# A two-layer graph kernel: z taken from x itself, W0 applied where z is turned, and the first four rows of z accumulated side by side

## What is computed

```
A = adj (4096 x 4096), x (4096 x 128)
scale = sum over k of d[k] * filt[k] * d[k]                 # one number per row
x1  = layernorm(x  + A @ (scale * (A @ (x @ W0))) + bias)
z2  = (A / rowsum(A)) @ x1 @ W_in;  y = (A.T / colsum(A)) @ x1 @ W_out
out = layernorm(x1 + z2 + y)
```

## Time and profile before

| | |
|---|---|
| median of 3 runs | 744.5 us (744.1 to 745.57) |
| profiled execution, its own time | 744.1 us |
| its span, by the profile | 742.3 us |
| PE busy | 732.4 us (99%) |
| weight loads busy | 606.3 us (82%) |
| DVE busy | 551.9 us (74%) |
| ACT busy | 476.1 us (64%) |
| POOL busy | 1.9 us |
| moved by DMA | 208.64 MB, mean 281 GB/s |
| granted TensorE clock, mean | 0.997 |

### The profile page before, as it was taken

How to read it: one execution, slowest core, us unless ns; L and a number is a source line. 1 busy time by engine, 2 the same in 40 slices (tenths; PEclk the granted TensorE clock), 3 DMA queues, 4 the chain that set the end, 5 groups by cost and what they waited for, 6 DMA issues and landing times.

```text
span 742.3 us, 9053 instructions
## 1 busy us (share of the span) xinstructions
PE 732.4 (99%) x3337; PEld 606.3 (82%) x3337; DVE 551.9 (74%) x669; ACT 476.1 (64%) x1167; POOL 1.9 (0%) x8
## 2 busy tenths in 40 slices
PE   8999999999999999999999999999999999999996
PEld 6878888888888888888888888888888888888885
DVE  5896865838474455887665647988897999899996
ACT  6897673837264534334343346999998888777772
POOL 0000000000000000000000000000000000000000
PEclk9999999999999999999999999999999999999998
DMA  9998875765556446255555559999989999999991
GB/s 367 394 367 349 358 268 215 260 220 205 217 202 226 158 182 226 87 206 209 179 177 217 173 191 377 385 384 383 378 328 385 386 371 373 375 365 354 352 357 34
DMA packets 35244, 208.64 MB, mean 281 GB/s; under 512 B 3584, under 2 KB 8448, under 8 KB 10752
## 3 DMA queue, kind: packets, MB, share of 16 engines
q1 hardware_dynamic: 34640, 207.34, 74.2%
q10 hardware_dynamic: 560, 0.72, 0.3%
HBM read 205.95 MB, written 2.10 MB: 280 GB/s over the span
## 4 chain that ended last, share of the span: by engine, by line
PE 95%; ACT 2%; DVE 1%; DMA 1%; issue 0%; SPq 0%; DVEq 0%
PE accA L594 15%; PE accA L591 15%; PE accA L600 15%; PE accB L591 12%; PE accB L594 12%; PE accB L600 12%; PE accC L594 4%; PE accC L591 4%; PE accC L600 4%; PE nat L615 2%; ACT hi L280 2%; PE nat L622 1%; PE nat L632 1%; DMA raw<-in_adjT_b 1%; DVE rows L503 0%
## 5 line engine op out<-in xcount | busy, mean ns | idle before, releaser
L398 DVE TENSOR_TENSOR lo<-raw,hi 128x2048 fp32r<-128x2048 f32 x184 | 417.4, 2288 | 134.6 <-ACT hi L280 103.0
L280 ACT ACTIVATE hi<-raw 128x512 fp32r<-128x512 f32 x512 | 315.6, 620 | 65.4 <-DMA raw<-in_adjT_b 37.9
L591 PE MATMUL accA<-hi,x_hi 128*128 128x512 f32 x512 | 201.5, 394 | 0.8 <-ACT x_hi L288 0.8
L594 PE MATMUL accA<-hi,x_lo 128*128 128x512 f32 x512 | 199.5, 390 | 0.3 <-DVE x_lo L403 0.3
L283 ACT ACTIVATE hi<-raw 128x2048 fp32r<-128x2048 f32 x64 | 122.1, 1912 | 66.9 <-DMA raw<-in_adjT_b 66.8
L600 PE MATMUL accA<-lo,x_hi 128*128 128x512 f32 x512 | 137.1, 390 | 0.6 <-DVE lo L398 0.6
L591 PEld LDWEIGHTS accA<-hi,x_hi 128*128 128x128 f32 x512 | 96.2, 188 | 20.9 <-ACT x_hi L288 1.1
L600 PEld LDWEIGHTS accA<-lo,x_hi 128*128 128x128 f32 x512 | 95.9, 188 | 21.0 <-DVE lo L398 1.1
L594 PEld LDWEIGHTS accA<-hi,x_lo 128*128 128x128 f32 x512 | 96.2, 188 | 19.8 <-DVE x_lo L403 0.6
L591 PE MATMUL accB<-hi,v_hi 128*128 128x512 f32 x256 | 100.5, 393 | 0.2 <-DVE v_lo L432 0.2
L594 PE MATMUL accB<-hi,v_lo 128*128 128x512 f32 x256 | 99.7, 389 | 0.0
(11 more groups left out here) (72 smaller groups left out, 462.6 us busy)
## 6 DMA issues: line engine op xcount, KB each, us to landing
raw<-in_adjT_b SPq DMA_DIRECT2D x127, 1024.0 KB, 5.4
raw<-in_adj_b SPq DMA_DIRECT2D x64, 1024.0 KB, 6.0
rows<-in_xT_b SPq DMA_DIRECT2D x8, 256.0 KB, 8.8
rows<-in_x_t SPq DMA_DIRECT2D x8, 256.0 KB, 6.9
out<-rows SPq DMA_DIRECT2D x7, 256.0 KB, 7.1
raw<-in_adjT_b SPq DMA_DIRECT2D x1, 512.0 KB, 5.3
raw<-in_adjT_b ACTq DMA_DIRECT2D x1, 512.0 KB, 5.4
out<-rows SPq DMA_DIRECT2D x1, 128.0 KB, 1.8
```

The source lines that it names most:

```text
L280: nc.scalar.activation(hi[slot][:, t], raw[slot][:, t], ACT.Copy, accum_out=sums[:, TPB * K + t, C:C + 1]).then_inc(s_hi, 1)
L398: nc.vector.tensor_tensor(lo[slot][:], raw[slot][:], hi[slot][:], ALU.subtract).then_inc(s_lo, 1)
L591: nc.tensor.matmul(acc, r_hi[:, TPB * K + t], h[:, t], start=(first and t == 0), stop=False)
L594: nc.tensor.matmul(acc, r_lo[:, TPB * K + t], h[:, t], start=False, stop=False)
```

## The change

1. `x_w0`, `xT_b`, the loads of `xT_b` and the later load of `x_t` go. Each block of x is loaded once (`load_x`), and x itself is split. ACT makes `x_hi` (`x_first`), POOL makes `x_lo`; DVE does both for block 0 (`x_start`).
2. At turning, z is multiplied by W0 (`by_rows(I, w0)`) where it was transposed. `v_block` is divided: ACT makes `v_hi` (`v_first`, four scaled 128x128), DVE makes `v_lo` with four fused instructions.
3. Rows 0 to 3 of z (LEAD = 4) run in step: for each block J of x, the chunks (J, 0), (J, 1), (J, 2), (J, 3), into four accumulators. The last two J come row by row. These 32 chunks give z only. The row sums are not taken there.
4. The 10 o products of those rows with J <= I move to phase 2, whose list gets 10 more chunks ("alone": they give an o product and nothing else), set between those that give o and y ("both"). The sums of A are taken in phase 2 instead: there every chunk is split tile by tile.
5. The first two chunks are loaded by tile (three tiles of them from ACT's queue), the next 14 in halves; `lo` of the first 32 chunks is made in quarters or halves.
6. Semaphore counts, positions and the place of one `inverse` follow.

```
+LEAD = 4
-    phase1 = [((I + 1 + k) % NB, I) for I in range(NB) for k in range(NB)]
-    phase2 = [(J, I) for I in range(NB - 2, -1, -1) for J in range(NB - 1, I, -1)]
+    lead = [(J, I) for J in range(NB - 2) for I in range(LEAD)]
+    lead += [(J, I) for I in range(LEAD) for J in (NB - 2, NB - 1)]
+    phase1 = lead + [((I + 1 + k) % NB, I) for I in range(LEAD, NB) for k in range(NB)]
+    phase2 = []
+    for I in range(NB - 2, -1, -1):
+        both, alone = list(range(NB - 1, I, -1)), list(range(I + 1)) if I < LEAD else []
+        while both or alone:
+            if alone:
+                phase2.append((alone.pop(0), I))
+            if len(both) > 1 or not alone:
+                phase2.append((both.pop(0), I))
...
-    y_behind = {N1 + 3: [N1]}
-    for n in range(N1 + 4, N2):
+    both = [n for n in range(N1, N2) if chunks[n][0] > chunks[n][1]]
+    y_behind = {both[3]: both[:1]}
+    for n in both[4:]:
         done = sum(len(m) for m in y_behind.values())
-        many = 2 if n == N1 + 6 else 1
-        y_behind[n] = list(range(N1 + done, N1 + done + many))
+        many = 2 if n == both[6] else 1
+        y_behind[n] = both[done:done + many]
...
+    turn1 = {28: 0}
+    for I in range(1, NB - 1):
+        turn1[LEAD * NB + I if I < LEAD else last1[I] + 2] = I
+    v_from = {n + 2: turn1[n] for n in turn1}
...
+    TILEWISE, HALVES = range(2), range(2, 4 * LEAD)
+    parts = [TPB if n in TILEWISE else 2 if n < LEAD * NB else 1 for n in range(N4)]
...
+        z_acc = [accA[:, 0], accA[:, 1], accC[:, 0], accC[:, 1]][:LEAD]
+        z_acc += [accA[:, I % 2] for I in range(LEAD, NB)]
...
+            def load_x(b):
+                sp.dma_start(rows[:, block_of(b)], x_t[:, block_of(b)]).then_inc(s_x[b], 16)
...
+            def v_first(I):
+                if I == 0:
+                    act.wait_ge(s_sc, 1)
+                act.wait_ge(s_n, I + 1)
+                for t in range(TPB):
+                    row = TPB * I + t
+                    last = nc.scalar.activation(v_hi[:, row], nat[:, I % 2, P * t:P * t + P], ACT.Identity,
+                                                scale=scale[:, row:row + 1])
+                last.then_inc(s_vhi, 1)
...
+            def x_first(b):
+                act.wait_ge(s_x[b], 16)
+                nc.scalar.activation(x_hi[:, block_of(b)], rows[:, block_of(b)], ACT.Copy).then_inc(s_xhi, 1)
...
+            for b in range(1, NB):
+                pool.wait_ge(s_xhi, b)
+                nc.gpsimd.tensor_tensor(x_lo[:, block_of(b)], rows[:, block_of(b)], x_hi[:, block_of(b)],
+                                        ALU.subtract).then_inc(s_xlo, 1)
...
             def v_block(I):
+                dve.wait_ge(s_vhi, I + 1)
                 for t in range(TPB):
+                    row = TPB * I + t
+                    last = nc.vector.scalar_tensor_tensor(v_lo[:, row], nat[:, I % 2, P * t:P * t + P],
+                                                          scale[:, row:row + 1], v_hi[:, row], ALU.mult, ALU.subtract)
+                last.then_inc(s_v, 1)
...
             def turn_z(I):
                 pe.wait_ge(s_tz, I + 1)
                 if I == 0:
                     pe.wait_ge(s_small, 16 * len(small))
-                transposes(NAT_Z + I, I)
+                by_rows(I, w0)
```

More of the change, by code:

```diff
@@ L88, in graph_kernel @@
     for n in range(N1):
-        if chunks[n][0] != chunks[n][1] and n not in HELD:
+        if not held(n):
             ranked(n)
         if n in diag1:
-            ranked(NB * diag1[n] + NB - 1)
+            ranked(last1[diag1[n]])
     for n in HELD + [N1 - 1]:
@@ L95, in graph_kernel @@
     for n in range(N1, N2):
+        if n not in both:
+            ranked(n)
         for m in y_behind.get(n, []):
@@ L105, in graph_kernel, with with_sums @@
         slot = n if n < RING else slot_of[order[n - RING]]
-        landings[slot] += 16 if n else 0
+        landings[slot] += 0 if n in TILEWISE else 16
         slot_of.append(slot)
         landed.append(landings[slot])
+    def with_sums(n):
+        J, I = chunks[n]
+        return J <= I and I >= LEAD if n < N1 else n < N2 or is_z2[n]
     hi_at, lo_at = [], []
@@ L269, in _, with split @@
         def _(act):
-            def split(n, tiles=range(TPB)):
+            def split(n):
                 slot = slot_of[n]
                 K, C = chunks[n]
-                if n:
+                if n not in TILEWISE and n not in HALVES:
                     act.wait_ge(s_raw[slot], landed[n])
-                if n < N1 or is_z2[n]:
-                    for t in tiles:
-                        if n == 0:
-                            act.wait_ge(s_piece[t // 2], 16)
+                if with_sums(n):
+                    to = sums[:, 1 if is_z2[n] else 0]
+                    for t in range(TPB):
@@ L280, in split @@
                         nc.scalar.activation(hi[slot][:, t], raw[slot][:, t], ACT.Copy,
-                                             accum_out=sums[:, TPB * K + t, C:C + 1]).then_inc(s_hi, 1)
+                                             accum_out=to[:, TPB * K + t, C:C + 1]).then_inc(s_hi, 1)
+                elif n < LEAD * NB:
+                    for t in range(TPB):
+                        if n in TILEWISE:
+                            act.wait_ge(s_tile[n][t], 16)
+                        elif n in HALVES and t == 0:
+                            act.wait_ge(s_half[slot], landed[n])
+                        elif n in HALVES and t == 2:
+                            act.wait_ge(s_raw[slot], landed[n])
+                        nc.scalar.activation(hi[slot][:, t], raw[slot][:, t], ACT.Copy).then_inc(s_hi, 1)
@@ L587, in product, with by_hi @@
                 h, l = hi[slot_of[n]], lo[slot_of[n]]
-                for t in range(TPB):
+                def by_hi(t):
                     if t == 0 or hi_at[n][t] > hi_at[n][t - 1]:
@@ L621, in transposes @@
                     to = slice(P * t, P * t + P)
-                    mm = nc.tensor.transpose(nat[:, e % 2, to], turned[:, u % 2, to], ident[:])
-                mm.then_inc(s_n, 1)
-            def x_w0(n):
-                b = chunks[n][0]
-                pe.wait_ge(s_xT[b], 16)
-                if n == 0:
-                    pe.wait_ge(s_w0, 16)
-                room(n)
-                for t in range(TPB):
-                    mm = nc.tensor.matmul(nat[:, n % 2, P * t:P * t + P], rows[:, TPB * b + t], w0[:],
-                                          start=True, stop=True)
+                    mm = nc.tensor.transpose(nat[:, e % 2, to], turned[:, e % 2, to], ident[:])
                 mm.then_inc(s_n, 1)
```

271 lines of the change are left out of this document (138 added, 133 removed).

## The result

The changed kernel takes 746.95 us (median of 10 runs, 745.74 to 747.98), the one before 744.49 (10 runs beside them, 743.93 to 745.57): ratio 1.0028, 95% interval 1.002 to 1.0036. It is 2.5 us slower by the medians. I had forecast 741.5, with 0.12 for slower; 746.95 lies above my range. The profiled run took 745.86 us with a span of 743.7, against 744.1 and 742.3 before. What lies outside the span is 2.1 us here and was 1.8 before, so it isn't the same for both kernels as I had written: 0.3 us of the difference lies there.

The account below looks back on a forecast made before the run. PE was taken to bound the kernel. PE's work -2.9, lead -3.4, stall +3.4 gave -2.9 us, less 0.3 for the slow clock: -2.6 on 744.1, so 741.5 us, range 737.0 to 746.0.

Parts of the forecast that it names:

- the lead: First 32 chunks, one product each: 6.7 us of PE time lost where 10.1 were lost before, a gain of 3.4.
- slow clock at the start: Start of the run: 0.3 us left for PE's slow clock when it begins earlier.
- my formula: Lead: landing is 4 us, plus bytes beyond 0.68 MB at 418 GB/s, plus 0.7; chunk 23 lands at 67.7, ends 71.5.
- four chunks with an x block: Lead: their transfers take 10.7 us against PE's 10.9, so the lag hardly grows.
- -6.3 us of PE's work: Row 0: removing x W0 from PE counted as a saving of 6.3 us.
- PE's work, -2.9: Whole run: x W0 gone, -6.3 us; eight z blocks rise from 0.48 to 0.91, +3.4; sum -2.9 us.
- The stall at chunk 71: Phase 2: PE waits 3.4 us for `lo`, because DVE makes x1 of block 5 first.
- The later rows of phase 2: x1 of rows 4, 3, 2 ends before `lo` is wanted, two places with 1.0 us to spare: nil, bound +2.
- The transfers' steady rate: Lead: transfers deliver 418 GB/s with full queues, as in the trace from 4 to 28 us.
- POOL's `x_lo`: Lead: about 1.3 us per operation; delays to DVE cost 0.5 us, bounds 0 and 4.
- Rival 2: Lead served worse, by 395 GB/s transfers or POOL's 4 us: 3.6 us later, 745.1, no change; chance 0.21.
- Rival 3: Lead bound by transfers in earnest, 370 GB/s: 8.1 us late, 749.6, slower; chance 0.12.

Follow-up runs that it names:

- e12: e7 with ident, bias, w_out and w_in (0.26 MB) loaded behind chunks 36 to 39 instead of 18 to 21: 741.62 us, ratio 0.9954 to the kernel before.
- e7: Changed kernel with (7,3) first in row 3 of phase 2, x1 of block 4 and its square root one chunk earlier, `x_lo` on DVE: 742.37 us.
- e9: The kernel before without three of the four x W0 tiles of blocks 2 to 7, 4.1 us less PE work: 743.62 us, ratio 0.9984.
- e11: The kernel before without sums in the first 16 splits and without three of four x W0 tiles of blocks 2 to 7: 743.32 us, ratio 0.9976.
- e10: The kernel before without the sums in ACT's first 16 splits, x W0 whole: 743.17 us, ratio 0.9981.
- e3: Changed kernel with LEAD = 0: W0 at turning and quick start stay, phase 1 goes row by row: 745.76 us, ratio 1.0012 to the kernel before.
- e1: Changed kernel with (7,3) first and (0,3) second in row 3 of phase 2: 744.15 us, ratio 0.999 to the kernel before.
- e4: Changed kernel with `x_lo` of blocks 1 to 7 made by DVE instead of POOL, all bytes loaded: 746.58 us, ratio 1.0018 to the kernel before.
- e2: Changed kernel with chunks 6 to 31 loading two of their four tiles, each read twice: 756.84 us, ratio 1.0153 to the kernel before.
- e6: Changed kernel with chunks 6 to 31 loading two of four tiles and `x_lo` on DVE: 743.79 us, ratio 0.9983 to the kernel before.

## Why the prediction was wrong

**The step that failed** is the lead: "The lead costs 6.2 + 0.5 = 6.7 us of lost PE time", set against 10.1 before, a gain of 3.4. Its mechanism held (PE is fed by the transfers, at 419 GB/s behind the first 10 us, and its lost time stands behind the last block of x), its size did not: 11.0 us were lost, a cost of 0.9. 8.0 of them were there at product 4, where my numbers gave 6.2, and 3.0 were added up to product 25, where they gave nothing. In the profiled run the sum is then 741.5 + 4.3 (lead) + 0.1 (stall) - 0.3 (slow clock at the start, which did not come) + 0.3 (outside the span) = 745.9; it took 745.86. The parts of the 4.3, worked out at chunk 24, for which my formula gives a landing at 4 + (25 x 1.0486 + 8 x 0.262 - 0.68)/0.418 + 0.7 = 70.8 and an end at 74.6, 6.6 us lost (I had stopped at chunk 23, with 6.2):

- The first 10 us brought 0.48 MB less than I put: 1.15 us. I had taken the start's rates from another set of transfers, the kernel before's, and no tile of it was loaded by itself. No run isolates this term. I had also put PE's first matmul at 5.0 (5.60), but the transfers covered that.
- The small loads, 0.42 MB, go out with chunks 16 to 21, inside the stretch; I had counted them for chunk 34 only: 1.0 us. e12 shows it for 0.26 of the 0.42 MB.
- A landing is later than its bytes' turn. By 74.06 the stretches had moved 0.57 + 2.14 + 7.5 + 13.4 + 6.0 = 29.6 MB, and up to chunk 24 they needed 28.7: 0.9 MB of later chunks were in before it, 2.1 us, where I had allowed 0.7. That is 1.4, worked out, not isolated by a run.
- Between landing and PE's end 5.1 us instead of 3.8: 1.3. POOL, for which I had left 0.5, has 0.8 of them (e7 against the changed kernel): its `x_lo` and the operation queued behind it.
- The rate was 419 to 425 where I had 418, which gives back 0.35.

1.15 + 1.0 + 1.4 + 1.3 - 0.35 = 4.5, and 6.6 + 4.5 = 11.1, where 11.0 were measured. To my 6.7 that is 4.5 + 0.4 (chunk 24 for 23) - 0.5 (allowed for POOL) = 4.4.

**The reason behind it** is a sentence of mine: "four chunks with an x block take (4.19 + 0.26)/0.418 = 10.7 us and PE 10.9". At 98% use there is next to no reserve. What is late stays late, and I had added up only the delays that I could name at the start. The kernel before had a reserve: x W0 made row 0's pace 3.62 us a chunk against 3.13 of transfers. So "-6.3 us of PE's work" was an accounting that held for PE's work and not for the time: with 4.1 us of it taken away e9 won 1.2 us by its ratio and 0.3 by its span, and e11 nothing that shows against e10. e3 took all of it away and lost, though DVE and ACT's order had a share there. e9 also shows that the reserve was not lost evenly: 2.8 us were won up to product 7, and the landing of chunk 8 took them back.

**Right by its own steps.** PE's work, -2.9: measured. The stall at chunk 71, 3.4 us by DVE's order, with x1 of block 5 ahead of it: 3.5, and e1 takes it away. What I had no term for is the clock behind such a stall, 1.6 us more in e4's execution. The later rows of phase 2, which I put at nil: nothing more was lost there. But "at two places with 1.0 us to spare" held only for that order; e1 opened one of them for 1.7 us. The transfers' steady rate: 418 against 419 to 425. The slow clock at the start: the profile of the changed kernel has 1.00 in all stretches shown, so nothing for my 0.3.

**POOL's `x_lo`.** I had 1.3 us from the width of the row; it is 1.27 when DVE leaves it alone (the shortest in e2) and 1.81 to 2.22 beside it in the changed kernel. The Trainium skill (SBUF — State Buffer, "Who interferes with whom"), which I cited for two engines that shut each other out for an instruction, names what e4, e7 and e2 show; but I had thought of DVE as the loser in the main, and in e2 it is POOL, for 20 us.

**The rivals.** Rival 2, the lead served worse, came nearest, with a price of 3.6 us where 4.3 was true; of its two causes neither came as written (the rate was 357 GB/s from 4 to 10 us and not low all along, and POOL cost 0.8), and I had given it 0.21. The chances failed because of that: a sum that lives on a resource at 98% should have its own case of delays that add up, with more weight than the case in which all goes to plan. Rival 3's 370 GB/s did not come in the lead. What I held against it was in part wrong: "in those 22 us the ring was full and loads waited for releases" does not fit 28 to 30 us, where 199 GB/s were moved with chunks 8 to 10 already issued. Two small slips: at 428 GB/s the lead would be 1.5 us shorter, not 1.1, and at 391 it would be 4.3 longer, not 4.1; neither changes the forecast.

**The median and its spread.** The profiled run is 1.1 us faster than the median, and only so does the median lie above my range. The ten runs of the changed kernel spread from 745.7 to 748.0, those of e7 from 742.2 to 742.8. They fall in two groups: five with a mean granted clock of 0.997 took 745.7 to 746.7, five with 0.993 to 0.996 took 747.2 to 748.0. e4 shows the same two groups, at 744.7 to 745.2 and 746.2 to 747.6, and its profiled run, of the second, has the clock of 0.57 behind the stall. So the second group of the changed kernel is probably the same thing; that is argued, for its profile is of the first group. Within either group the changed kernel is about 0.9 us behind e4, which agrees with the 0.8 of POOL. It would also explain why e1 won 2.8 us and not only the 1.8 by which its stall is shorter. Terms below 1 us are known from one or two executions each, for the leads of the changed kernel and of e1 differ by that much.

## What to carry to other kernels

Work that a trace shows on the bounding engine is worth its time only where that engine is the bound; in a stretch that the transfers pace it may be nearly free, and an experiment that leaves most of it out (e9) tells so at the price of one run. Where a plan runs a resource above 95%, sum every byte and every delay in the stretch, the small loads too, since none is made good later; then move out what can wait (e12). When chunks are reordered, go through the order of each engine again for who stands ahead of what: here the first stall of phase 2 was found on paper, the second in e1's profile, and mending both was most of the gain (e1, e7). Do the same for an edit that is meant as an experiment: e3's put ACT and DVE in the way.

## What the runs showed of the hardware

- POOL and DVE with two inputs each do not share evenly. With DVE making one subtraction behind the other, one 128x512 subtraction of POOL took 20.4 us instead of 1.27 (DVE idle) or 1.81 to 2.22 (the changed kernel), and PE waited 11.3 us for it (e2). The other way round DVE's 128x1024 halves took 1.3 to 1.8 us beside POOL instead of 1.22, and up to 2.3 in e3.
- Behind a wait of PE of 2.16 us at chunk 71 the granted clock stayed at 1.00 in one execution (the changed kernel) and was 0.57 over the next 4 us in another (e4), with matmuls 0.43 us apart instead of 0.23; that cost 1.6 us. Around the wait of 11.3 us in e2 it was 0.77 and 0.55 in two stretches of 10 us.
- In e3, e6 and e12 the first 28 us had stretches of 0.80 to 0.97, and e12 was nevertheless the fastest of all.
- With queues kept full, a transfer of 512 KB took a median of 12.0 us from issue to landing, against 4.9 for the 1024 KB chunks over the run; the rate was 419 to 425 GB/s for 80 us. In the first 10 us, with loads of single tiles, it was 357 GB/s from 4 to 10 us, against 411 in the kernel before.
